# Attention's hand-written order of work: later steps for a hyperbolic chain, other starts for its eight units, earlier row maxima and tighter projections

## The reference

```python
qkv = x @ qkv_w.T                                   # rotary on q and k
outs.append(_sdpa(q[:, :6], k[:, :6], v[:, :6], 1.0 / math.sqrt(HD)))
outs.append(_hyp_attn(q[:, 6:10], k[:, 6:10], v[:, 6:10], curvature))
outs.append(_sdpa(qn, kn, v[:, 10:], math.sqrt(HD)))
y = concat(outs) @ proj_w.T + proj_b
# _hyp_attn, per head:
arg = jnp.maximum(-curv * inner, 1.0 + 1e-07)
dis = jnp.sqrt(1.0 / curv) * jnp.arccosh(arg)
scores = 1.0 / (eps + dis) + causal_bias
# then:
x = layernorm(x + attention(x))
x = layernorm(x + ffn(x))      # 8 experts, top 2
```

## Time and profile before

| | us |
|---|---|
| median of 3 runs | 2009.93 |
| lowest to highest | 2007.54 to 2014.39 |
| the profiled execution's own time | 2006.02 |
| its span in the trace | 2004.4 |
| projection stage | about 0 to 277 |
| eight attention turns | 277.2 to 1720.4 |
| tail and experts | 1720.4 to 2004.4 |

### The profile page before, as it was taken

How to read it: one execution, slowest core, us unless ns; L and a number is a source line. 1 busy time by engine, 2 the same in 40 slices (tenths; PEclk the granted TensorE clock), 3 DMA queues, 4 the chain that set the end, 5 groups by cost and what they waited for, 6 DMA issues and landing times. The chain is left out here.

```text
span 2004.4 us, 38754 instructions
## 1 busy us (share of the span) xinstructions
PE 1614.2 (81%) x13082; PEld 910.1 (45%) x13082; DVE 1196.0 (60%) x3014; ACT 1387.3 (69%) x1456; POOL 754.7 (38%) x369
## 2 busy tenths in 40 slices
PE   8999847877977997798689779977977896628993
PEld 4665513433433443444344334433443443418993
DVE  5877746535865775576568657665865775521013
ACT  3665648986887888788788978987897888401110
POOL 3334434343443543443343335334343655300003
PEclk9999969978998998999899889988998998859997
DMA  4699741452055005504420650254055101149862
GB/s 169 198 245 291 217 126 33 99 88 47 2 86 138 14 13 95 119 12 73 98 67 2 107 119 12 34 95 108 2 86 132 44 21 43 43 184 412 314 232 74
DMA packets 66080, 215.18 MB, mean 107 GB/s; under 512 B 16945, under 2 KB 26801, under 8 KB 57105
## 3 DMA queue, kind: packets, MB, share of 16 engines
q1 hardware_dynamic: 56704, 179.35, 35.4%
q0 software_dynamic: 9200, 33.43, 5.6%
HBM read 144.14 MB, written 68.58 MB: 106 GB/s over the span
## 5 line engine op out<-in xcount | busy, mean ns | idle before, releaser
L1152 ACT ACTIVATE a_PT<-a_s 128x1024 f32<-128x1024 f32 (+3 forms) x576 | 459.8, 810 | 151.4 <-PE a_s L971 86.4
L1230 POOL TENSOR_TENSOR a_Z<-a_Z,a_R 128x2182 f32<-128x2182 f32 x64 | 290.1, 4534 | 451.8 <-ACT a_R L1164 445.0
L968 PE MATMUL a_s<-Q,K 96*128 96x512 bf16 (+7 forms) x1152 | 329.1, 350 | 105.2 <-ACT a_PT L1152 75.6
L1227 POOL TENSOR_TENSOR a_R<-a_Z 128x2182 f32<-128x2182 f32 x64 | 245.0, 3828 | 244.1 <-DVE a_Z L1342 206.4
L1350 DVE TENSOR_REDUCE a_mx<-a_w 128x1 f32<-128x512 f32 (+2 forms) x576 | 307.4, 550 | 45.6 <-PE a_w L996 39.2
L983 PE MATMUL a_o<-a_PT,a_V 128*32 128x512 f32 (+3 forms) x2304 | 268.8, 541 | 79.3 <-ACT a_PT L1152 48.2
L1342 DVE TENSOR_SCALAR_CACHE_REDUCE a_Z<-a_w 128x512 f32<-128x512 f32 (+7 forms) x384 | 202.9, 528 | 112.5 <-PE a_w L1011 66.4
L1028 PE MATMUL a_w<-a_ident,a_R 128*128 128x128 f32 (+1 forms) x1152 | 207.4, 307 | 39.4 <-DVE a_PTh L1396 21.3
L1396 DVE COPY a_PTh<-a_w 128x512 f32<-128x512 f32 (+1 forms) x256 | 158.4, 622 | 109.8 <-PE a_w L1028 107.5
L996 PE MATMUL a_w<-K,Q 96*128 96x512 bf16 (+2 forms) x576 | 188.5, 333 | 28.4 <-DVE a_mx L1350 12.0
L968 PEld LDWEIGHTS a_s<-Q,K 99*128 99x128 bf16 (+1 forms) x1152 | 110.8, 103 | 200.6 <-ACT a_PT L1152 110.8
(11 more groups left out here) (164 smaller groups left out, 2530.0 us busy)
## 6 DMA issues: line engine op xcount, KB each, us to landing
e_w<-in_w SPq DMA_DIRECT2D x23, 2048.0 KB, 8.5
qk_parts<-p_parts SPq DMA_DIRECT2D x128, 192.0 KB, 3.3
Q<-qk_parts SPq DMA_DIRECT2D x144, 128.0 KB, 5.3
K<-qk_parts SPq DMA_DIRECT2D x144, 128.0 KB, 8.0
v_rows<-p_vt SPq DMA_DIRECT2D x8, 2048.0 KB, 9.7
a_V<-v_rows SPq DMA_DIRECT2D x32, 512.0 KB, 9.4
p_xT<-in_xt SPq DMA_DIRECT2D x8, 1024.0 KB, 8.0
a_X<-in_x POOLq DMA_DIRECT2D x8, 1024.0 KB, 13.2
```

Of the source, the lines that this page charges most:

```text
L968: m = pe.matmul(sB[x % 2][:, i, 0:w], Kb[0:r, h, P * j:P * j + P], Qb[0:r, h, t0:t0 + w], start=True, stop=not diag)
L1152: act.activation(PT[:, u % 2, 2 * k:2 * k + 2, 0:w], sB[x % 2][:, :, 0:w], ACT.Exp, scale=scale_of(GROUPS[g][2 * k])).then_inc(prob.sem, 1)
L1227: pool.tensor_tensor(r, z, z, ALU.mult).then_inc(z_sq.sem, 1)
L1230: pool.tensor_tensor(z, z, r, ALU.add).then_inc(z_sum.sem, 1)
```

## The change

The order tables of a turn are replaced. In the chain of a unit, with `square` at slot r: `log_distance` goes from r + 15 to r + 18, `inverse` from r + 17 to r + 20, `row_bias` from r + 19 to r + 23, the four `hyp_exp` from r + 20, 22, 24, 26 to r + 24, 25, 29, 30, the turns of the two parts from r + 27 and r + 32 to r + 33 and r + 35, and `hyp_values` from r + 38 to r + 40. `log_square`, `root`, `add_root` and `log_sum` stay at r + 4, 6, 8, 13. The starts r were 12, 29, 46, 64, 81, 99, 116, 134 and are now listed. The arguments' spread is by unit. The first round of maxima runs over steps 1 to 6 (it was 2 to 8), the second over 8 to 18 (9 to 20). `turn_rows`, `project` and `statistics` have listed slots, 39 to 88 in place of 38 to 102. Some single items move by one to three slots. No item is added or removed, and no instruction changes its shape or buffer.

```diff
-        LEAD, SPAN = 12, 122
...
-        for n in range(NU):
-            ready = LEAD + SPAN * n // (NU - 1)
+        READY = (9, 33, 49, 65, 85, 101, 117, 136)
+        SPREAD = (8, 3, 2, 2, 2, 1, 2, 2)
+        CHAIN = (('square', 0), ('log_square', 4), ('root', 6), ('add_root', 8), ('log_sum', 13), ('log_distance', 18), ('inverse', 20), ('row_bias', 23))
+        for n, ready in enumerate(READY):
...
-            span = 2 * len(args) if n else 8
+            span = SPREAD[n] * len(args) if n else SPREAD[n]
...
-            put(ready + 15, ("log_distance", n))
-            put(ready + 17, ("inverse", n))
-            put(ready + 19, ("row_bias", n))
-            for k in range(4):
-                put(ready + 20 + 2 * k, ("hyp_exp", n, k))
-            for part, turned in ((0, 27), (1, 32)):
+            for kind, at in CHAIN:
+                put(ready + at, (kind, n))
+            for k, at in enumerate((24, 25, 29, 30)):
+                put(ready + at, ("hyp_exp", n, k))
+            for part, at in enumerate((33, 35)):
...
-        ROUNDS = (((4, 5), 1, 2, 7), ((0, 1, 2, 3), 2, 9, 12))
+        ROUNDS = (((4, 5), 1, 1, 6), ((0, 1, 2, 3), 2, 8, 11))
...
-            put(38 + 8 * k, ("turn_rows", n))
-            put(42 + 8 * k, ("project", n))
+            put(ROWS[k], ("turn_rows", n))
+            put(PROJECT[k], ("project", n))
...
-        for at, item in ((25, ("shift",)), (104, ("variance", 0)), (106, ("inverse_root", 0)),
-                         (112, ("newton", 0)), (114, ("normalize", 0, 0)), (115, ("normalize", 0, 1)), (116, ("mid_out",)),
-                         (121, ("add_bias",)), (123, ("statistics", 1, 0, NT // 2)), (124, ("statistics", 1, NT // 2, NT)),
-                         (125, ("variance", 1)), (126, ("inverse_root", 1)), (129, ("newton", 1)),
-                         (131, ("normalize", 1, 0)), (132, ("normalize", 1, 1)), (133, ("rows_out",)), (141, ("rows_in",))):
+        for at, item in ((25, ("shift",)), (104, ("variance", 0)), (106, ("inverse_root", 0)), (114, ("newton", 0)), (114, ("normalize", 0, 0)), (114, ("normalize", 0, 1)), (115, ("mid_out",)), (120, ("add_bias",)), (122, ("statistics", 1, 0, NT // 2)), (124, ("statistics", 1, NT // 2, NT)), (126, ("variance", 1)), (127, ("inverse_root", 1)), (129, ("newton", 1)), (130, ("normalize", 1, 0)), (131, ("normalize", 1, 1)), (134, ("rows_out",)), (141, ("rows_in",))):
```

More of the change, by code:

```diff
@@ L731, in put @@
             work[at // NSLOT][at % NSLOT].append(item)
-        for n in range(NU):
-            ready = LEAD + SPAN * n // (NU - 1)
+        READY = (9, 33, 49, 65, 85, 101, 117, 136)
+        SPREAD = (8, 3, 2, 2, 2, 1, 2, 2)
+        CHAIN = (('square', 0), ('log_square', 4), ('root', 6), ('add_root', 8), ('log_sum', 13), ('log_distance', 18), ('inverse', 20), ('row_bias', 23))
+        for n, ready in enumerate(READY):
             args = [("argument", n, k, pc) for k, seg in enumerate(segments(n)) for pc in range(len(seg[3]))]
-            span = 2 * len(args) if n else 8
+            span = SPREAD[n] * len(args) if n else SPREAD[n]
             for a, item in enumerate(args):
                 put(ready - span + a * span // len(args), item)
[L739 to L743, removed]
-            put(ready + 15, ("log_distance", n))
-            put(ready + 17, ("inverse", n))
-            put(ready + 19, ("row_bias", n))
-            for k in range(4):
-                put(ready + 20 + 2 * k, ("hyp_exp", n, k))
-            for part, turned in ((0, 27), (1, 32)):
+            for kind, at in CHAIN:
[3 more added lines that the diff above has]
+            for part, at in enumerate((33, 35)):
                 for q in range(len(turns(n, part))):
-                    put(ready + turned + q, ("turn", n, part, q))
+                    put(ready + at + q, ("turn", n, part, q))
             if n % 2:
                 for part in range(2):
-                    put(ready + 38 + part, ("hyp_values", HYP_TILES[n - 1 + part]))
-        ROUNDS = (((4, 5), 1, 2, 7), ((0, 1, 2, 3), 2, 9, 12))
+                    put(ready + 40 + part, ("hyp_values", HYP_TILES[n - 1 + part]))
+        ROUNDS = (((4, 5), 1, 1, 6), ((0, 1, 2, 3), 2, 8, 11))
         MAXIMA = [[(h, i, pc, s0, w) for h in hs for i in range(NT) for pc, (s0, w) in enumerate(pieces(i))]
@@ L762, in attend @@
                                         if m * steps // len(MAXIMA[r]) == u])
-            work[first_step + steps][1].append(("join_maxima", r))
+            work[first_step + steps][0].append(("join_maxima", r))
             work[first_step + steps][3].append(("turn_maxima", r))
```

7 lines of the change are left out of this document (4 added, 3 removed).

## The result

The median is 2090.96 us (4 runs, 2084.0 to 2097.71) against 2011.95 for the kernel before beside it (4 runs, 2007.54 to 2014.39): a ratio of 1.040, 95% interval 1.036 to 1.044. The forecast was 1983, and its range ended at 2014. The change is slower, by three times what rival A had priced.

The account below looks back on a forecast made before the run. It took a turn as ACT's 151.6 us of work plus 29.3 us of holes. Terms summed to -3.7 us a turn: -26 over seven turns, -3 first turn, +2 tail, total -27, so 2009.9 became 1983 us; overall range 1949 to 2014.

Parts of the forecast that it names:

- rival A: First argument of each turn: the load lands later than 23.9 us after the last argument; 2037 us, chance 0.13.
- The three holes at the turn's end: Slots 127 to 5: waits before `log_square` of unit 7, exponential (0,0) and `log_sum` of unit 7 close: -3.3, -1.6, -1.8.
- I take the 20.2: Turn's start: SP's load was taken to last 20.2 us from PE's last argument to the next batch's first.
- The hole before exponential (0,1): Turn's start: ACT waits while PE's argument waits for the load; 8.0 us in place of 1.26, +6.7.
- Slots 104 to 124: Slots 108 to 124: `mid_out` ahead of `square` saves 3.5 us of DVE; holes fall to 1.0 us, -4.2.
- Slots 4 to 16: Slots 6 to 16: crowded PE and DVE work beside short exponentials; holes 1.1 become 3.4 us, +2.3.
- slots 39 to 48: Holes of 2.76 and 1.24 become 1.5 and 3.1 us, +0.6; 6.2 instead of 4.6 without PE's lead.
- slots 88 to 104: PE goes to the low clock from about slot 94, before nine argument and turn items; holes 1.7 become 3.0, +1.3.
- Slots 16 to 38: Slots 16 to 30: the hole of 1.98 us behind three exponentials in a row closes, -2.0.
- Rival B: Turn's start and slots 88 to 95: PE idles, then runs longer at 1.2 GHz; 2007 us, chance 0.12.
- `inverse_root` of the rows: `inverse_root` 1: the store of `mid_out` leaves some 2.4 us earlier, so its wait falls from 2.1 to 0.5, -1.6.
- The end: Tail after the turns: `add_root` of unit 7 and two `hyp_exp` join the wrapped items, +2 us.

Follow-up runs that it names:

- in_args_late: The changed kernel with the load of rows (`rows_in`) at slot 12 of the next turn and unit 0's arguments at slots 4 to 11: 2038.6 us, ratio 1.0172.
- in_late: The changed kernel with the load of rows (`rows_in`) moved from slot 141 to slot 12 of the next turn: 2050.9 us, ratio 1.0241.
- norm_behind: in_args_late with both pieces of the normalising at slot 115, behind DVE's copy of the output bank, and `mid_out` at 116: 2017.5 us, ratio 1.0034.
- before_mid: The kernel before with the second normalising piece at slot 114 and `mid_out` at 115, ahead of `square` of unit 6: 1994.8 us, ratio 0.9946.
- mid_behind: The kernel before with the normalising and `mid_out` at slot 115, behind the output bank's copy, ahead of `square` of unit 6: 1993.9 us, ratio 0.9906.
- start_norm: norm_behind with unit 7 two slots earlier, at 134: 1999.8 us, ratio 0.9924.

## Why the prediction was wrong, point by point

**What held.** The view was right: ACT's work stayed, and the time is that work plus its holes. The three holes at the turn's end (6.7 us) closed to 0.3 us. One of them, `log_sum` of unit 7, stays closed only while ACT waits for the load ahead of it: in in_args_late it waits 1.3 us for POOL again. Slot 62 holds 1.1 us (forecast 3.0), slots 64 to 88 0.7 (1.0). PE did come to `K<-t_parts` with scores queued behind it.

**The step that failed most** is the sentence "I take the 20.2: five of the six waits share 6.9 us, so they are alike", with the argument against rival A, "that the load starts at the same distance from POOL's store as before". Both read the load's 20.2 us as a property of the load. It was one of the order: POOL's store came 4.5 us after the trigger, and the 1 MB load of rows 16.0 us after. The new order put the store 1.9 us ahead of it and so the load of rows 5.5 us after it. The hole before exponential (0,1) became 16.3 us on average instead of 8.0. Seven turns of 8.3 us are 58; taking that transfer away gave 40 in in_late, whose own first two loads still came late. With a load of 18.3 us the forecast's working gives 6.1 us, and in_late measured 6.3. With the change's mean of 27.2 us it gives 15.0, and 16.3 was measured: the last argument also ran up to 2 us later against ACT than worked out. So the chain of steps was sound, and 7 of the 8.3 us come from its one wrong input. Rival A had the late landing, with 27.9 us, and was given 0.13; it didn't say what made the load late, and its 2037 lacked the terms below.

**Slots 104 to 124, booked at -4.2.** Measured: 3.5, where batch 3 had 5.2 before, the mean of the turns 4.4; a gain of 0.9 to 1.7. The forecast counted 3.5 us of DVE's time saved, and not what stands behind the normalising on DVE. The time was saved (2.67 us for eight tiles), but the wait for `newton` and the eight tiles together held the output bank's copy. norm_behind puts this queue at 21 us in all. What it cost in the kernel before isn't separated: before_mid halved PE's wait for the copy, mid_behind ended it, and the two take the same time.

**Places where PE is the bound.** Slots 4 to 16 were forecast at 3.4 us and measured 5.3, slots 39 to 48 at 4.6 and 6.7, slots 88 to 104 at 3.0 and 4.7. In the first and the last PE is busy 15.64 of 16.00 and 10.37 of 10.40 us, at a granted clock of 0.82 and 0.73: it has no slack at all, and starts low (0.50 from 1238 to 1243 us and from 1350.6 to 1356). In slots 39 to 48 no clock is lost (1.00 from 1284 to 1295 us); there 6.7 is just above the forecast's bound of 6.2 for a PE without any lead. There the forecast had given PE a lead that it didn't have. For slots 4 to 16 it had booked all of the 3.4 us by which its count of PE's work, 9.7 us, exceeded ACT's, so the count was too low; for slots 88 to 104 it had no bound at all. Slots 16 to 38 were to lose a hole of 2.0 us and hold 1.9 on average: four holes of 0.4 to 0.7 in place of the one.

**Rival B, the clock.** The granted clock of the whole attention part fell from 0.92 to 0.85, and the stretches behind PE's long waits stand at 0.50 to 0.52. The page of the Trainium skill that the forecast weighed (TensorE: Matmul & The Clock Gate, Part 1) has the low clock as the default that only activity lifts; the rows agree. But norm_behind keeps the low clock at slot 116 (values of 1.94 us) and loses nothing there. For the same work PE was busy 155.33 us a turn instead of 149.08, but how much of that lies on the path, and so what the low clock costs of the 79 us by itself, was not separated by any run.

**The rest.** `inverse_root` of the rows waits 1.6 us (0.5 forecast), though the store of `mid_out` leaves 18.2 us ahead of it instead of 13.4. The store isn't what it waits for. It is the last operation of `variance` on DVE, and that ends when POOL's `add_root` of unit 6 does:

```profile
1390.99 4.83 POOL L1222 TENSOR_TENSOR a_Z<-a_Z,a_R 128x2182 f32<-128x2182 f32 x1 [8.50 <-ACT a_R L1156]
...
1392.55 3.30 DVE L1456 TENSOR_SCALAR a_rs<-a_mv 128x8 f32<-128x8 f32 x1
...
1395.88 0.21 ACT L1178 ACTIVATE a_rs<-a_rs 128x8 f32<-128x8 f32 x1 [1.60 <-DVE a_rs L1456]
```

In the kernel before it was the same: `add_root` ended at 976.91 us, the operation on DVE at 976.94, and `inverse_root` began at 976.97. The end, booked at +2 for wrapped items, is +7.7 us; the runs with unit 7 at 134 have 282 to 286 us there, those with 136 have 288 to 292. In sum a turn has 41.9 us of holes where 26 were forecast: half of the miss is the load, half the many small ones.

## What to carry to other kernels

A landing time read from a trace belongs to the order in which it was taken: list the transfers around it and what triggers each, and ask whether the edit moves one of them, before a wait is put in front of the critical engine. When an item is moved on an engine that has slack, look at what is queued right behind it and who waits for that; here holding up a 0.7 us copy cost 3 us a turn, more than the 2.7 us of normalising ahead of it. And where a stretch's PE work just equals its length, price it by the bound without lead.

## What the runs showed of the hardware

With a 1 MB load issued by POOL 4.4 us after SP's first of 24 small loads (5.5 us after the last argument), these landed 28.0 us after that argument; with it issued behind them, at the same boundary of in_late, 18.3. From 1209 to 1236 us the DMA engines were busy all the time:

```profile
1209.00:1236.00 27.00, 8.50 (x135) 5.84 (x134) 5.24 (x15) 10.93 (x11) 9.48 (x3) 0.69 1.04 187
```

The place of the 1 MB store may matter too. With it issued 0.5 us after the last argument the small loads took 16.8 to 18.3 us at four of in_late's boundaries, but 19.0 to 23.6 at the six of norm_behind; with it issued some 7 us after (start_norm, which differs from norm_behind by unit 7's place alone and has the store behind POOL's `square`) they took 23.7 to 24.3, with no load of rows beside them in any of these. What that spread hangs on was not tried, nor why the first boundary still took 26.1 us in in_late.

DVE's small operations were held up by POOL's long ones. Of the four tiles that took 4.89 us beside POOL's `square`, three took about 0.40 us each and one 3.91: it ended at 960.31 us, the `square` at 960.17. The last operation of `variance`, on 128x8 elements, took 0.17 us with no long operation of POOL beside it. Beside a 128x2182 TENSOR_TENSOR of POOL it took up to 3.58 in the change, and between 800 and 1420 us it ended each time within 0.03 us of POOL's end. Four tiles clear of POOL took 1.34 to 1.38 us.
